# The residual tiles enter the PSUM bank as transposes ahead of the output products, with a new stage order

## What is computed

```python
x = _layernorm(x + sa, g1, be1)        # sa = o @ wo + bo
x = _layernorm(x + ff, g3, be3)        # ff = gelu(x @ w1 + b1) @ w2 + b2
out = out.transpose(0, 2, 1, 3).reshape(B, Nq, D)
x = q_x + out @ Wo.T + bo
```

## Time and profile before

| | us |
|---|---|
| median of 3 runs | 3905.13 |
| the profiled execution | 3907.5 |
| its span, first to last instruction | 3905.7 |
| TensorE busy (matmul records) | 3784.1 |
| VectorE busy | 2345.0 |
| ScalarE busy | 2139.2 |
| GpSimd busy | 1141.6 |

### The profile page before, as it was taken

The page is one execution under the profiler, slowest core; times in us unless marked ns, Lnnn a source line. Parts: engine busy times, 40 slices in busy tenths (PEclk is TensorE's granted clock), DMA queues, the critical chain, the costliest instruction groups (busy, mean ns, idle before and its releaser), DMA issues.

```text
span 3905.7 us, 60616 instructions
## 1 busy us (share of the span) xinstructions
PE 3784.1 (97%) x22859; PEld 2075.3 (53%) x23156; DVE 2345.0 (60%) x5047; ACT 2139.2 (55%) x2751; POOL 1141.6 (29%) x1051
## 2 busy tenths in 40 slices
PE   5999999999999999999999999999999999999998
PEld 3645645555565554555565565455546456455553
DVE  2665576655675567565567547656556755756556
ACT  0565565555555556555555555655565654555455
POOL 2422332222442232222253123222234322312222
PEclk9999999999999999999999999999999999999999
DMA  5311221112231131121232122112123212212111
GB/s 201 111 52 50 88 81 49 60 54 88 81 96 41 58 109 51 49 79 47 90 100 77 36 79 90 42 55 74 55 92 99 95 50 79 66 33 71 50 52 49
DMA packets 259268, 281.26 MB, mean 72 GB/s; under 512 B 24979, under 2 KB 251155, under 8 KB 255379
## 3 DMA queue, kind: packets, MB, share of 16 engines
q1 hardware_dynamic: 257444, 276.58, 21.6%
q10 hardware_dynamic: 1536, 0.79, 0.1%
HBM read 196.79 MB, written 79.69 MB: 71 GB/s over the span
## 4 chain that ended last, share of the span: by engine, by line
PE 89%; DVE 5%; ACT 3%; issue 1%; POOL 1%; DMA 1%; SPq 0%; ACTq 0%; DVEq 0%; POOLq 0%
PE pv L670 14%; PE st L645 13%; PE mx L719 13%; PE mx L610 13%; PE st L697 8%; PE mx L587 8%; PE st L596 4%; PE mx L722 4%; DVE row_max L872 3%; PE mx L679 2%; PE st L735 2%; ACT probs L785 2%; PE st L624 1%; PE st L686 1%; DVE y L913 1%
## 5 line engine op out<-in xcount | busy, mean ns | idle before, releaser
L872 DVE TENSOR_REDUCE row_max<-mx 128x1 bf16<-128x512 f32 (+4 forms) x3072 | 1669.1, 595 | 583.6 <-PE mx L610 202.1
L785 ACT ACTIVATE probs<-st 128x1024 f32<-128x1024 f32 (+1 forms) x1344 | 1263.8, 977 | 620.5 <-PE st L645 393.0
L943 POOL TENSOR_TENSOR qm<-q_high,own_rows 128x512 bf16<-128x512 bf16 x768 | 792.0, 1039 | 1770.7 <-PE mx L610 859.2
L610 PE MATMUL mx<-k_high,qm 128*128 128x512 bf16 (+4 forms) x2775 | 814.3, 341 | 24.3 <-DVE row_max L872 14.5
L645 PE MATMUL st<-q_packed,k_packed 97*128 97x512 bf16 (+2 forms) x3072 | 807.9, 343 | 10.6 <-issue 4.5
L670 PE MATMUL pv<-probs,va 128*32 128x512 f32 (+2 forms) x6144 | 705.6, 531 | 19.1 <-ACT probs L785 15.0
L610 PEld LDWEIGHTS mx<-k_high,qm 128*128 128x128 bf16 x3072 | 284.7, 97 | 522.9 <-DVE row_max L872 194.9
L645 PEld LDWEIGHTS st<-q_packed,k_packed 97*128 97x128 bf16 (+1 forms) x3072 | 283.3, 98 | 320.8 <-ACT probs L785 73.9
L893 DVE TENSOR_TENSOR y<-mx,row 128x256 f32<-128x256 f32 x288 | 121.7, 423 | 531.0 <-PE mx L722 530.0
L719 PE MATMUL mx<-w2s,hid 128*128 128x256 f32 x1536 | 348.8, 380 | 0.4
L697 PE MATMUL st<-xT,w1s 128*128 128x512 f32 x768 | 341.6, 593 | 0.0
(11 more groups left out here) (88 smaller groups left out, 3556.6 us busy)
## 6 DMA issues: line engine op xcount, KB each, us to landing
k_packed<-k_parts_dram SPq DMA_DIRECT2D x576, 128.0 KB, 2.7
q_packed<-q_parts_dram SPq DMA_DIRECT2D x576, 128.0 KB, 2.7
q_parts_dram<-q_low SPq DMA_DIRECT2D x96, 256.0 KB, 2.1
k_parts_dram<-k_low SPq DMA_DIRECT2D x96, 256.0 KB, 2.1
w1s<-w_dram SPq DMA_DIRECT2D x12, 1024.0 KB, 4.9
w2s<-w_dram SPq DMA_DIRECT2D x12, 1024.0 KB, 7.2
q_parts_dram<-q_high SPq DMA_DIRECT2D x48, 256.0 KB, 2.1
k_parts_dram<-k_high SPq DMA_DIRECT2D x48, 256.0 KB, 2.1
```

What stands on the lines that cost most here:

```text
L610: mm = pe.matmul(bank[:, 0:k1 - k0], qm[:, h % RING, i * P:(i + 1) * P], high["k"][s][:, t, k0:k1], start=True, stop=(k_kind == FULL))
L785: act.activation(dst[:, :, 0:w], held["scores", b, a, n, e][:, :, 0:w], ACT.Exp, scale=ATT_SCALE[a]) \
L872: dve.tensor_reduce(row_max[s][:, i, h:h + 1], held["max", b, a, h, i][:, 0:k1 - k0], AX_X, ALU.max, negate=True).then_inc(*mx_drained.mar ...
L943: pool.tensor_tensor(qm[:, h % RING], high["q"][s][:, h // HT], own_rows[:, h % HT:h % HT + 1].to_broadcast([P, TOK]), ALU.mult) \
```

## The change

In a fill, the two operations on the carried tile move ahead of the output product and get the transpose flag. The first of them starts the bank; the output products no longer start it but add onto what it holds, and the last of them ends the group. For `pre` and `ctx`, which have no product, the two transposes are the whole fill. Waits, banks, signals and the stages themselves stay as they were. All 14 strings of `MERGE` are new; two of them are shown, and the others change in the same manner.

```diff
--- before.py
+++ after.py
@@ -222,36 +222,36 @@
 MERGE = {
-    "10": "010110212110121102121122122213210112300110101011101011101010010011110100101011010101121101011021"
-           "222223222022022020220022020222020202200022220202220202200000000",
+    "10": "002211101232113001212222213221011110101110111101010101110100011001111010010101121101011010210001"
+           "010122222222020022020220222022220202002020022220200220202202000",
 ...
-    "last": "011011020111211021001111210120102110101101101011001101010000111101010110101010011010101100212100"
-           "00000000022220000000200",
+    "last": "011011022111010100100111101011101011101000110110011211000111101021101011010001101001100101002100"
+           "20200000000220002000222",
 }
@@ -715,12 +715,13 @@
                         if i == 0:
                             pe.wait_ge(*st_drained.past(("hid", b, int(tag[1]), FT // 2 - 1)))
                     bank = held["rows", b, tag, i] = mx_bank()
-                    for j in range(count):
-                        pe.matmul(bank[:, 0:D], src[:, j, i * P:(i + 1) * P], weight[:, j, :], start=(j == 0), stop=False)
                     carried = cT[s] if tag == "ctx" else xT[s]
                     for j in range(KT):
                         mm = pe.matmul(bank[:, j * P:(j + 1) * P], carried[:, j, i * P:(i + 1) * P], eye[:],
-                                       start=(count == 0), stop=(count == 0 or j == KT - 1))
+                                       is_transpose=True, start=(j == 0), stop=(count == 0 and j == KT - 1))
+                    for j in range(count):
+                        mm = pe.matmul(bank[:, 0:D], src[:, j, i * P:(i + 1) * P], weight[:, j, :], start=False,
+                                       stop=(j == count - 1))
                     mm.then_inc(*mx_filled.mark(("rows", b, tag, i)))
                 elif kind == "turn":
                     tag, half = stage[2:]
```

More of the change, by code:

```diff
@@ L231 @@
[L231 to L240, removed]
-           "0",
-    "40": "010110201121110211000212122202200110221111230331000011033223131112331111032032222130121322221101"
-           "210210110221021022220110020121112110210222222220200202202202022022020220022020000022220202022220"
-           "20",
@@ L245 @@
[L245 to L250, removed]
@@ L251 @@
-    "00": "111100111101120111110111101110111211112113101101011100111011101100110121323333322223332330300030"
-           "333303033300320233330033000333330333303300230000",
-    "last": "011011020111211021001111210120102110101101101011001101010000111101010110101010011010101100212100"
-           "00000000022220000000200",
+    "first": "022001110011110111001111111111111111101110010101111011000111011101110110010222222222220222000222"
+           "2022202222022002022220222000222000",
+    "01": "111101121010113101110111121111211101112121321022102120121101100111201110112110100102022222322220"
+           "00222022020200222002220002220002022202200222022",
@@ new lines @@
+    "10": "002211101232113001212222213221011110101110111101010101110100011001111010010101121101011010210001"
+           "010122222222020022020220222022220202002020022220200220202202000",
+    "11": "011011022111012110222221021201011001100221121110121112122002120110100112110012222002011201102110"
+           "11010010110121022222202222220202202202022202022202002020022222022200220200000",
+    "20": "010021211012111011222221021201112211101211011101110110110002222001202122222010201011011011100011"
+           "0211012102012210222222222220222020220222002020222022002022220222002202",
@@ new lines @@
+    "21": "011021322111302110110222210212011122111010111101011011100101001111121100120011101011011000110012"
+           "2222003222200222200220222000202220220200222202220200222",
+    "30": "002211101232113001212222213221011110101110111101010101110100011001111010010101121101011010210001"
+           "010122222222020022020220222022220202002020022220200220202202000",
+    "31": "011011022111012110222221021201011001100221233330333121121113111011223113001112101012212122211020"
+           "230020022022212332121200111210100200012222222220002202202202202022022000220200000222202022202220"
+           "0",
@@ new lines @@
+    "40": "011011022111012110222221021201011001100221233330333121121113111011223113001112101012212122211020"
+           "230022002202221233212120011121010020001222222222000220220220220202202200022020000022220202220222"
+           "00",
+    "41": "011011022111010321103200011112101112210121110210111211121223001111201010121102101100212110210110"
+           "2103222222220202002022200022200200222020022020000022222000220202202000",
+    "50": "011011022111010321103200011112101112210121110210111211121223001111201010121102101100212110222101"
+           "102103222222220202002022200022200200222020022020000022222000220202202000",
@@ new lines @@
+    "51": "011011030110101011001112010111010110110001101001112110120011110101101011010001101001100101000133"
+           "3333033333303330003330333003333003233033333033303320022222302223",
+    "00": "000300221101011211110121112221210111101100111120111101100111110111011230112002011101011001333323"
+           "333333033330333303333033003303333303330003330030",
+    "last": "011011022111010100100111101011101011101000110110011211000111101021101011010001101001100101002100"
+           "20200000000220002000222",
```

## The result

The changed kernel takes 3798.87 us (median of 4 runs, 3796.65 to 3800.73) against 3905.07 us before: a ratio of 0.9728, 95% interval 0.9711 to 0.9745. That is 106.2 us faster, where the prediction said 80 (3825 us), with a range of 3800 to 3860. The profiled execution took 3800.11 us, with a span of 3798.3 us.

A forecast was written before the change was run, and what follows sets the result against it. TensorE's instruction issue was taken as the bound, its matmul row 97% busy. The terms -154.9 + 77.4 + 15.8 - 23.4 + 5 = -80.1 us gave 3825 us at the median's level, with an 8-in-10 range of 3800 to 3860.

The forecast's parts named there:

- The swap of records: In 352 row fills, identity products out (-154.9 us) and fp32 transposes in (+77.4 us), saving 77.4 us.
- The mechanism of the order: On TensorE, 117 fewer entries into narrow-tile stages at 0.2 us each, saving 23.4 us.
- slower: Rival, in the fills: transposes don't pipeline, each taking its whole 0.278 us record; 3928 us, chance 0.02.
- the other (3887): Rival, in the fills: the flag leaves two records of 0.11 us per tile, so only the order counts; chance 0.02.
- the step from transpose to product: In 288 fills, a product behind a transpose on its bank costs 0.055 us more: 15.8 us, between 0 and 49.
- waits that grow: TensorE's waits on VectorE's maxima and ScalarE's exponentials, put at 45 us, grow by 5; bounds nothing or about 40.
- the order gives more: Rival: the new order of stages also hides half of today's 45 us of TensorE waits; about 3800 us, chance 0.10.

The follow-up runs named there:

- the additional products: Kernel before plus one bf16 product in each of 96 hidden stages: 3939.75 us on a 128x32 weight tile, 3917.49 on a full 128x128 one.
- the doubled transposes: New fills in the old order of stages, each fill's two transposes issued twice: 3899.58 us, against 3831.56 with them once.
- the run without it: Old fills and new order, with values, row-maxima and out stages moved behind the next loop's load: 3859.77 us, against 3873.49 for the new order alone.
- the run without the flag: Kernel before, old order, with the identity products moved ahead of the output products and no transpose flag: 3907.14 us, ratio 1.0004.
- out stage moved: Changed kernel with the second out stage of the 00 loops moved four places later, behind the load stage: 3795.27 us, ratio 0.9717.

## Why the prediction was wrong

**Right.** TensorE's stream is the bound, and a microsecond taken from it is one of the time: the two parts came out as 74.1 and 32.2 us and add up. The swap of records (-154.9 + 77.4) holds, as 704 records of the old pace and as 74 us in the run. The mechanism of the order, fewer entries into narrow tiles, holds with its price: 0.19 us from the trace and 0.23 from the additional products, 22 to 27 us where 23.4 stood. The rivals in which the transposes were slow or weren't transposes are out: slower (3928) by the 0.22 us in the timeline and by the doubled transposes, the other (3887) by the record count.

**Wrong: "the step from transpose to product"**, 15.8 us. It is zero: 0.22 us from two transposes to the first product. The rows I bounded it with the earlier trace rows had a turn ahead of products of another stage, on another bank, and I read their 0.17 and 0.08 us as the price of a step. They aren't. The run with the new fills in the old order has transposes behind those turns, nothing switches there, and the distance is the same 0.61 us:

```profile
582.07 0.60 PE L736 MATMUL st<-eye,y 128*128 128x128 f32 x4
582.68 0.41 PE L720 MATMUL mx<-eye,cT 128*128 128x128 f32 x2
```

It is there in all eight such places of that run, and the 0.08 in the same four. With the new order and the old fills, fp32 products follow a turn in 16 places, and in all of them the first starts 0.11 us behind the last transpose, as between two transposes. So the distance belongs to the old order of stages. In both rows three L610 stages stand directly ahead of the turn, which take all three `mx` banks, so a wait for VectorE to free a bank is my reading (at the first row the first of its three reductions starts at 593.40 and takes 0.69 us, and the fill starts at 594.24); no run tests it alone.

**Wrong: "waits that grow"**, +5 us. I argued from the shorter fills, and for them it is right that little comes back (0 to 3 us: 77.4 against 74.1, within the interval). But the same table that saves the narrow runs also places the stages against VectorE and ScalarE. With the old fills and the new order TensorE's waits on the exponentials and maxima fell by 11.7 and 7.7 us, 19.4 together. What I had as a rival of 10% ("the order gives more") is what happened, by the side of a wait that I had not seen at all: the late load, some 13 us with its half clock, a term that the sum put at nothing.

The order's account is then -22 to -27 (narrow runs) - 19.4 (waits, from the list) + 13.7 (late load, from the run without it) = -28 to -33, and measured is -32.2. It is an account from separate readings, and the measured times in it are uncertain by some 6 us each, so its closing proves no single term. The whole lists of waits say the same: behind the start-up, those of the old order come to 43.3 us (the run without the flag), those of the new order with the old fills to 33.7, of which 9.9 are the late load.

Together: the two terms were off by 15.8 and, for the order, by 32.2 - 18.4 = 13.8 us, less 3.3 us of the swap that the run didn't show: 26 us, and the range ended 1 us too high. Its lower end took in the free step or an order that gives more, each alone, not both. That the range missed by so little is luck: without the late load, which I hadn't seen either, the time would have been some 12 us lower.

A point of the Trainium skill against the change was that transposes might cost 275 ns and not hold the clock ("TensorE: Matmul & The Clock Gate", "PE-mode transpose"). The pace is not this case's: 0.11 us apiece, with 275 ns only as the length of a record. On the clock the runs say less. It was 1.00 in the stretch from 1250 to 2200 us, which holds 336 of them now in these two lines where the earlier trace rows counted those of the turns alone:

```profile
1250.00:2200.00 950.00, 33.04 (x176) 22.54 (x176) 1.00 0.23 74
...
1250.00:2200.00 950.00, 25.10 (x160) 17.91 (x160) 1.00 0.23 74
```

The first line is L720 alone, the second L736. The clock does fall in this stretch for some microseconds at 1990, but after an idle time, as shown above. These transposes are 58 us of busy records among 950 us of other work, so whether transposes alone would hold the clock no run here shows.

## What to carry to other kernels

Where a residual is added on TensorE by an fp32 product with an identity, the transpose flag halves it, ahead of the products or behind them. When the order of a program whose TensorE is full is changed, count the steps between narrow and full weight tiles in the list before anything else, and then follow each load back to the operation that it waits for, on each queue that it passes: a load 3 us late can cost more than its wait. Before a distance between two starts is taken as the price of a step, look for the same distance where nothing switches; if it is there too, it is something else. A table of order changes waits of both signs, so a term "waits grow" needs a bound on both sides.

## What the runs showed of the hardware

- An fp32 128x128 transpose with the flag adds onto a bank and may be added onto: 0.11 us a record (the same product without the flag is two records, 0.22 us), no step cost from transpose to product in 288 of 288 fills.
- A bf16 product of 128 columns on a 128x32 weight tile between full ones cost 0.36 us of the kernel's time (34.1 us over 96), on a full tile 0.12 (11.8 over 96), though the records are 0.23 and 0.22 us long. At the kernel's own narrow stages the trace has 0.09 us to enter and 0.10 to leave.
- After idle times of 3.12 and 3.34 us TensorE's clock stood at 1.2 GHz for some 5 and 3.4 us of work. Shorter ones went both ways: it fell after 1.69 us (new order alone) and 2.03 (out stage moved), and not after 1.59 (changed kernel), 2.26 (out stage moved) and 2.55 (new order alone).
